# A graph layer over sorted edges: another order of loads, one-hots, clears and weight splits in the first twenty-odd microseconds

## The reference, cut to what matters

```python
h   = maximum(layernorm(x), 0)
agg = segment_sum(edge_attr, dst, 12500)        # 48 features per node
c   = concatenate([h, agg], axis=1)
h1  = silu(c  @ W1 + b1)                        # 176 -> 256
h2  = silu(h1 @ W2 + b2)                        # 256 -> 256
out = x + h + (h2 @ W3 + b3)                    # 256 -> 128
```

## Time and profile before

| | |
|---|---|
| median of 3 runs | 303.75 us |
| the profiled execution | 302.05 us |
| its span | 300.3 us |
| TensorE busy | 283.9 us (95%) |
| VectorE busy | 249.2 us (83%) |
| ScalarE busy | 222.5 us (74%) |
| GpSimd busy | 112.2 us (37%) |
| data moved | 54.49 MB, mean 181 GB/s |
| GB/s in the 7.5 us slices 1 to 6 | 171, 293, 264, 242, 170, 215 |

### The profile page before, as it was taken

The page is one execution under the profiler, slowest core; times in us unless marked ns, Lnnn a source line. Parts: engine busy times, 40 slices in busy tenths (PEclk is TensorE's granted clock), DMA queues, the critical chain, the costliest instruction groups (busy, mean ns, idle before and its releaser), DMA issues.

```text
span 300.3 us, 12188 instructions
## 1 busy us (share of the span) xinstructions
PE 283.9 (95%) x4370; PEld 256.4 (85%) x4371; DVE 249.2 (83%) x615; ACT 222.5 (74%) x434; POOL 112.2 (37%) x243
## 2 busy tenths in 40 slices
PE   7596879999999999999999999999999999999995
PEld 3584758899999999999999999999999999999794
DVE  7956988799888898889988898889988889875551
ACT  5555267887788877888777887888777887789662
POOL 4062345243433435334343334434444343542200
PEclk9899599999999999999999999999999999999999
DMA  6998999368655786557855678556875568631112
GB/s 171 293 264 242 170 215 253 85 204 244 192 164 156 228 244 177 161 158 237 243 162 151 182 240 233 157 155 189 244 232 151 150 203 244 199 109 34 33 32 58
DMA packets 79418, 54.49 MB, mean 181 GB/s; under 512 B 2997, under 2 KB 78863, under 8 KB 79253
## 3 DMA queue, kind: packets, MB, share of 16 engines
q1 hardware_dynamic: 79397, 54.25, 64.9%
HBM read 46.29 MB, written 6.40 MB: 175 GB/s over the span
## 4 chain that ended last, share of the span: by engine, by line
PE 78%; issue 8%; ACT 4%; POOL 3%; DMA 2%; DVE 1%; POOLq 1%; SPq 1%; ACTq 0%; DVEq 0%
PE agg_ps L1054 18%; PE z L1122 16%; PE z L1104 7%; PE z L1105 7%; PE z L1108 7%; PE agg_ps L1057 4%; PE z L1084 4%; PE z L1089 3%; PE z L1085 3%; PE z L1086 3%; PE z L1090 3%; POOL agg_carry L462 3%; PE tp L1068 3%; DMA raw<-in_edge_attr_dram 2%; ACT xn L543 1%
## 5 line engine op out<-in xcount | busy, mean ns | idle before, releaser
L462 POOL TENSOR_TENSOR agg_carry<-staged,agg_carry 48x42 f32 x196 | 69.5, 354 | 91.4 <-ACT staged L511 58.3
L1054 PEld LDWEIGHTS agg_ps<-onehot,raw 128*48 128x48 f32 x1560 | 75.2, 128 | 12.6 <-issue 12.5
L1054 PE MATMUL agg_ps<-onehot,raw 128*48 128x42 f32 x1560 | 78.9, 218 | 3.9 <-DVE onehot L729 3.7
L1057 PE MATMUL agg_ps<-onehot,raw 128*48 128x42 f32 x1568 | 79.3, 218 | 0.6 <-DMA raw<-in_edge_attr_dram 0.6
L729 DVE TENSOR_TENSOR onehot<-window,rel 128x1176 f32<-128x1176 f32 (+1 forms) x57 | 76.9, 1350 | 3.0 <-DVE stats L704 2.7
L1057 PEld LDWEIGHTS agg_ps<-onehot,raw 128*48 128x48 f32 x1568 | 75.8, 129 | 0.8 <-issue 0.8
L443 POOL TENSOR_TENSOR rstd<-vareps,minus_half 112x4 f32<-112x4 f32 (+1 forms) x28 | 39.5, 1411 | 77.4 <-DVE vareps L714 77.4
L1122 PE MATMUL z<-w,h 128*112 128x128 f32 (+1 forms) x448 | 55.9, 278 | 0.8 <-ACT h L575 0.8
L1122 PEld LDWEIGHTS z<-w,h 128*112 128x112 f32 (+1 forms) x448 | 50.4, 176 | 2.4 <-ACT z L571 1.1
L575 ACT ACTIVATE h<-z,b2c 128x448 f32<-128x448 f32 (+1 forms) x56 | 35.4, 633 | 20.3 <-PE z L1108 17.7
L543 ACT ACTIVATE xn<-x_t,nmr,rstd 112x128 f32<-112x128 f32 (+1 forms) x112 | 45.6, 478 | 0.9 <-DVE nmr L722 0.8
(11 more groups left out here) (128 smaller groups left out, 421.6 us busy)
## 6 DMA issues: line engine op xcount, KB each, us to landing
raw<-in_edge_attr_dram SPq DMA_DIRECT2D x55, 672.0 KB, 6.0
x_t<-in_x_dram SPq DMA_DIRECT2D x27, 224.0 KB, 6.3
out_dram<-out_t SPq DMA_DIRECT2D x27, 224.0 KB, 6.1
agg_carry<-agg_carry SPq DMA_DIRECT2D x3, 504.0 KB, 12.8
dst_rows<-in_dst_dram SPq DMA_DIRECT2D x1, 512.0 KB
raw<-in_edge_attr_dram SPq DMA_DIRECT2D x1, 288.0 KB, 3.5
dst_rows<-in_dst_dram SPq DMA_DIRECT2D x1, 256.0 KB, 2.8
out_t<-in_L_gnn_W_dram SPq DMA_DIRECT2D x1, 256.0 KB, 7.4
```

The costliest lines, as they stand in the source:

```text
L462: pool.tensor_tensor(into, staged[:, parity, n, :], into, ALU.add).then_inc(s_added, 1)
L1054: mm = pe.matmul(banks[0:ED, bass.ds(offsets[at - first], WINDOW)], edges, into, start=False, stop=True, skip_group_check=True, tile_posit ...
L1057: mm = pe.matmul(stage[ROW2:ROW2 + ED, at * WINDOW:(at + 1) * WINDOW], edges, into, start=(at == 0 and j == 0), stop=True, skip_group_chec ...
```

## The change

Ten edits, all in the beginning:

1. SP loads both halves of batch 0's edges ahead of index blocks 1 to 3; half 1 came behind them.
2. W1's loads stay where they were, W2's load moves behind the second half of batch 1's edges and the second tile of `x`, and each has its own semaphore.
3. The three copies of zeros (L384) go. GpSimd clears 16 more tiles of `agg_carry` in 4 memsets of 1,792 columns, right behind its last `iota` (L436), and ScalarE clears the last 10 with the overhang in one operation of 4,544 columns in place of two (2,752 and 896).
4. GpSimd reads the node numbers of batches 0 and 1 ahead of its first add, adds all 7 staged groups of batch 0, then computes the first `rstd`, then adds batch 1, then computes the second `rstd`. Before, `rstd` 0 came after 3 adds, and batch 1 was read and added in step 1, behind `rstd` 1.
5. VectorE makes both one-hots of batch 1 right behind those of batch 0, ahead of the check.
6. TensorE runs 5 warm-up products between the first offsets and the sum of batch 0, and turns index block 1 behind that sum and not ahead of it; 8 warm-up products, not 6, stand ahead of the sum of batch 1.
7. ScalarE copies the staged sums of batch 0 ahead of `rel_of(1)`; the high part of W2 is split behind the first normalisation.
8. VectorE splits W1's low part ahead of the first shift and W2's in step 1, behind the one-hots of batch 2.
9. The statistics of tile 1 are taken ahead of step 1; the second half of batch 2's one-hots comes ahead of the shift.
10. The waits for W2 and for the constants stand at their first users.

```diff
-    WARM0, WARM1 = 3, 6
+    WARM0, WARM1, WARM2 = 3, 5, 8
...
-        COPIED, COPIES = 6 * TILE, 3
-        ZEROED = 4 * TILE
+        ZEROED = 18 * TILE
+        CARRY0 = 2 + (ZEROED - POOL_ZEROS) // (4 * TILE)
...
-            load_edges(0, 0, 0)
+            for half in range(2):
+                load_edges(0, 0, half)
             sp.dma_start(dst_rows[:, 1:FULL_ROWS, :], rows[:, 1:FULL_ROWS, :]).then_inc(s_dst, 16)
...
-            load_edges(0, 0, 1)
             load_x(0, 0)
             load_edges(1, 1, 0)
-            sp.dma_start(w2_in, W2.rearrange("(m p) n -> p m n", p=P)).then_inc(s_weights, 16)
...
             load_edges(1, 1, 1)
+            load_x(1, 1)
+            sp.dma_start(w2_in, W2.rearrange("(m p) n -> p m n", p=P)).then_inc(s_w2, 16)
...
-            for c in range(COPIES):
-                sp.dma_start(zeros_to[:, c, :], agg_carry[:, ZEROED + COPIES * COPIED:NT * TILE]).then_inc(s_carry0_dma, 16)
...
             pool.iota(tile_i[:, :], pattern=[[1, TILE]], base=0, channel_multiplier=0).then_inc(s_pool_zero, 1)
+            for a in range(POOL_ZEROS, ZEROED, 4 * TILE):
+                pool.memset(agg_carry[:, a:a + 4 * TILE], 0.0).then_inc(s_carry0, 1)
...
             pool.wait_ge(s_off0, 1)
-            nodes = nodes_of(0)
-            pool.wait_ge(s_carry0, 2)
-            add_staged(0, 0, nodes, range(0, EARLY))
+            nodes = [nodes_of(b) for b in range(2)]
+            pool.wait_ge(s_carry0, CARRY0)
+            pool.wait_ge(s_carry0_act, 1)
+            add_staged(0, 0, nodes[0])
             rstd_of(0, 0)
-            add_staged(0, 0, nodes, range(EARLY, HALF))
+            add_staged(1, 1, nodes[1])
             rstd_of(1, 1)
...
-            clear_carry(ZEROED + COPIES * COPIED, NODES)
+            clear_carry(ZEROED, NODES)
...
-            clear_carry(POOL_ZEROS, ZEROED)
-            rel_of(1)
             stage_sums(0, 0)
-            for c in range(2, ROWS):
+            for c in range(1, ROWS):
                 rel_of(c)
...
             normalize(0, 0)
+            act.wait_ge(s_w2, W2_LOADS)
+            act.activation(w2_hi ...).then_inc(s_w_hi, 1)
             stage_sums(1, 1)
...
             make_onehot(0, 0, 1)
+            for half in range(2):
+                make_onehot(1, 1, half)
             dve.wait_ge(s_relrows, FULL_ROWS)
...
             aggregate_stats(0, 0)
-            make_onehot(1, 1, 0)
+            weights1_lo()
             shift_of_norm(0, 0)
-            make_onehot(1, 1, 1)
...
-            weights_lo()
+            load_stats(1, 1)
             dve.wait_ge(s_rel, ROWS)
...
                     agg_lo(0)
-                    load_stats(1, 1)
                     dve.wait_ge(s_stats, 2)
                     aggregate_stats(1, 1)
                     make_onehot(2, 0, 0)
+                    make_onehot(2, 0, 1)
+                    weights2_lo()
                     shift_of_norm(1, 1)
-                    make_onehot(2, 0, 1)
...
             pe.wait_ge(s_off0, 1)
+            for _ in range(WARM1):
+                pe.matmul(tp[:, 0:P], ident[:, :], ident[:, :], start=True, stop=True)
             offsets = offsets_of(0)
-            turn_rows(1)
             sum_tile(0, 0, offsets)
-            for c in range(2, ROWS):
+            for c in range(1, ROWS):
                 turn_rows(c)
...
-            for _ in range(WARM1):
+            for _ in range(WARM2):
                 pe.matmul(tp[:, 0:P], ident[:, :], ident[:, :], start=True, stop=True)
             sum_tile(1, 1, offsets)
```

More of the change, by code:

```diff
@@ L144, in gnn_kernel @@
         POOL_ZEROS = 2 * TILE
-        COPIED, COPIES = 6 * TILE, 3
-        ZEROED = 4 * TILE
-        assert ZEROED + (COPIES + 1) * COPIED == NT * TILE and LOOP[0] * TILE == ZEROED
+        ZEROED = 18 * TILE
+        CARRY0 = 2 + (ZEROED - POOL_ZEROS) // (4 * TILE)
+        assert (ZEROED - POOL_ZEROS) % (4 * TILE) == 0
         gen_onehot = onehot[:, 2:4].rearrange("p s e w -> p (s e w)")[:, 0:PER * TILE].rearrange(
@@ L451, in nodes_of, with add_staged @@
                 return nodes
-            def add_staged(b, parity, nodes, which=range(HALF)):
+            def add_staged(b, parity, nodes):
                 pool.wait_ge(s_staged, b + 1)
                 wait(pool, s_carried, b)
-                if isinstance(b, int) and b == LATE_ZEROS:
-                    pool.wait_ge(s_carry0_dma, 16 * COPIES)
-                for n in which:
+                for n in range(HALF):
                     wait(pool, s_added, added(b, n))
@@ L465, in step @@
                 parity = turn % 2
-                if has(i, 0, NT):
+                if has(i, 0, NT) and not (isinstance(i, int) and i == 1):
                     nodes = nodes_of(i)
@@ L579, in activate1 @@
                 n = PER * nodes_p(t)
+                if isinstance(t, int) and t == 0:
+                    act.wait_ge(s_const, CONSTS)
                 for m in range(M):
@@ L736, in make_onehot, with weights1_lo, weights2_lo @@
                 onehot_of(i, parity, half).then_inc(s_onehot, 1)
-            def weights_lo():
-                dve.wait_ge(s_w_hi, 4)
[L741 to L747, removed]
+            def weights1_lo():
+                dve.wait_ge(s_w_hi, 3)
+                dve.wait_ge(s_pool_zero, 3)
+                for lo, whole, hi in ((w1x_lo[:, :], w1x_in, w1x_hi[:, :]),
+                                      (w1e_lo[0:ED, :], w1e_in[0:ED, :], w1e_hi[0:ED, :])):
+                    dve.tensor_tensor(lo, whole, hi.bitcast(F32), ALU.subtract).then_inc(s_w_lo, 1)
+            def weights2_lo():
+                dve.wait_ge(s_w_hi, 4)
+                dve.tensor_tensor(w2_lo[:, :, :].rearrange("p m n -> p (m n)"), w2_in.rearrange("p m n -> p (m n)"),
+                                  w2_hi[:, :, :].rearrange("p m n -> p (m n)").bitcast(F32),
+                                  ALU.subtract).then_inc(s_w_lo, 1)
             dve.wait_ge(s_rel, 1)
@@ L857, in carry_over @@
                 dve.wait_ge(s_added, added(t + 1))
-                dve.wait_ge(s_carry0_act, 2)
-                if isinstance(t, int) and t == LATE_ZEROS - 1:
-                    dve.wait_ge(s_carry0_dma, 16 * COPIES)
+                if isinstance(t, int) and t == 0:
+                    dve.wait_ge(s_carry0, CARRY0)
+                    dve.wait_ge(s_carry0_act, 1)
                 wait(dve, s_carried, t)
@@ L1076, in layer1 @@
                 if isinstance(t, int) and t == 0:
[L1077 to L1080, removed]
+                    pe.wait_ge(s_w_lo, 2)
+                    pe.wait_ge(s_w_hi, 3)
                 for m in range(M):
@@ L1095, in layer2 @@
                 n = PER * nodes_p(t)
+                if isinstance(t, int) and t == 0:
+                    pe.wait_ge(s_w_lo, 3)
+                    pe.wait_ge(s_w_hi, 4)
                 pe.wait_ge(s_h1, M * t + M)
@@ L1116, in layer3 @@
                 last = isinstance(t, int) and t == NT - 1
+                if isinstance(t, int) and t == 0:
+                    pe.wait_ge(s_const, CONSTS)
                 pe.wait_ge(s_seeded, t + (2 if last else 1))
```

25 lines of the change are left out of this document (10 added, 15 removed).

## The result

| | kernel before | changed kernel |
|---|---|---|
| median of the runs, us | 303.84 (303.45 to 305.94, 4 runs) | 307.62 (307.10 to 307.84, 4 runs) |
| ratio to before, 95% interval | | 1.0133 (1.0096 to 1.0169) |
| profiled execution, us | 302.05 | 307.84 |
| its span, us | 300.3 | 306.1 |

1.3% slower.

A forecast was written before the change was run, and what follows sets the result against it. TensorE, gapless from 60 us, bounds the kernel, so the start of layer 1 of tile 1 counts: +5.4 (late S) - 2.0 (behind S) + 1.0 (clock) = +4.4 on 303.75 gives 308.2 us; range 304.3 to 310.8.

The forecast's parts named there:

- Which stall: VectorE's index chain: its fp32 `tensor_scalar`s stand while GpSimd's four new memsets run, shifting the chain by 6.0 us.
- let in between: Rival, VectorE's index chain: VectorE gets in between two memsets; shift 4.6 us, time 306.8 us; chance 0.20.
- The sign that I had named: VectorE's index chain: L643 or L644 lasts several us and ends near 10.
- The one-hots and the check: VectorE behind the index chain: one-hot 1 of batch 0 at 15.5, check entered at 19.4, over at 22.0.
- The offset rows: TensorE ahead of batch 1's sum: start between 22.0 and 23.3, taken as 22.6, after check and turned blocks.
- S: Moment TensorE has batch 1 summed: 23.63 before, forecast 29.0, 5.4 us late, bounds 4.8 and 6.6.
- Behind S: From batch 1's sum to layer 1 of tile 1: 16.2 us for 18.2, a gain of 2.0, bounds 2.5 and 1.2.
- The base of 15.7: VectorE's order behind S: 18.2 less statistics 0.87 and waits 0.91 and 1.37, plus W2's low part 0.67.
- the wait for `rstd`: VectorE's shift behind S waits for GpSimd's adds and `rstd`: between 0 and 1.3 us, taken as 0.5.
- The gap and the clock: TensorE idle 4.2 us ahead of layer 1 of tile 1; a clock fall behind it loses 0.8 to 2.5, taken 1.0.
- The step to the median: Whole kernel: the median lies 1.7 us above the profiled execution before; the same step put on the changed kernel.
- do not stall: Rival, VectorE's index chain: memsets do not stall it; -2.1 us, 301.7 us, 300.5 if the clock stays up; chance 0.14.

The follow-up runs named there:

- e2: Changed kernel with one GpSimd memset of 7,168 columns in place of four of 1,792: 308.33 us, 1.0160 of the kernel before.
- e5: Changed kernel with GpSimd waiting for the end of VectorE's index chain before its four memsets: 300.94 us, 0.9925 of the kernel before.
- e4: Kernel before with the new clearing alone (no copies, four memsets, one ScalarE clear), all orders as they were: 306.22 us, 1.0108 of the kernel before.
- e12: Kernel before with the new clearing alone, its four memsets waiting for the end of VectorE's index chain: 301.06 us, 0.9928 of the kernel before.
- e3: Changed kernel with sixteen GpSimd memsets of 448 columns in place of four of 1,792: 303.87 us, 0.9995 of the kernel before.
- e7: e5 with tile 1's statistics ahead of step 1 and the second `rstd` ahead of batch 1's adds: 298.69 us, 0.9868 of the kernel before.
- e1: Changed kernel with its four memsets put behind GpSimd's register loads of batches 0 and 1: 304.75 us, 1.0037 of the kernel before.
- e8: e6 and e7 together: 296.75 us, 0.9813 of the kernel before.
- e6: e5 with 12 unused TensorE products ahead of layer 1 of tile 1, two looped steps written out: 298.78 us, 0.9876 of the kernel before.

## Why the prediction came right, point by point

The measured 307.62 lies in the range and 0.6 us from the forecast of 308.2, with two errors that offset each other: that the median came so close is luck. Slower came as forecast, by the mechanism named, in the form of a rival.

- **Which stall (right) and its form (wrong).** The chain did shift because of the four memsets. But the forecast took them as one block of 6.0 us; the measured shift is 10.45 - 5.88 = 4.57, which is the rival "let in between" (4.6) to the digit, with the last stalled step L658 to L661. The sign that I had named, one operation of several us that ends near 10, did not come here; it came with the single memset (e2: 5.98 us, to 10.14). I had weighed against it that in the kernel before no stall ended at a boundary between memsets. That is still so: L639 again stands from 1.84 to 3.66 across several short memsets. Why those let nobody in, and memsets of 448 and of 1,792 columns do, stays open.
- **The one-hots and the check (right in order, 1.0 early).** The one-hot at 14.50 for 15.5, the check entered at 18.38 for 19.4 and over at 20.99 for 22.0. The smaller shift gives 1.4 of it; 0.4 was lost again between the first one-hot and the first offsets, for which VectorE waited 0.51 us for TensorE, then at 1.2 GHz.
- **The offset rows (wrong limit).** I had them at 22.6, from the check and the turned blocks together, 23.3 at most. They began at 23.57, 0.3 over that bound, set by the turned blocks alone: TensorE was at 1.2 GHz until 20.9 (0.53 in 10 to 20 us), and the five warm-ups took 2.50 us, for which the second set of eight took 2.05. I had priced the cold clock, but too low by 1 us. From there on the terms held: 23.57 + 1.64 + 2.05 + 2.7 = 29.96, measured 29.98. S was 6.35 late, forecast 5.4, inside the bounds.
- **Behind S (mis-sized).** 17.17 us, forecast 16.2. The base of 15.7 was right within 0.1, the wait for `rstd` was 1.58, not 0.5, and over the upper bound of 1.3. Rows of after show why: a GpSimd add of some 0.27 us took 3.21 beside two one-hots in a row and W2's split. The term was bounded by waits of the old order, in which the longest add took 1.73 us.
- **The gap and the clock (right, 0.5 short).** The gap was 4.11 us for 4.2, the clock fell behind it, and 1.5 us were lost (6.82 - 5.34) for 1.0.
- **What was not in the sum.** From the third `carry_over` to the end the changed kernel takes 252.5 us, before 253.5. Every kernel here has one of these two values within 0.3; what sets them is open. The sum against the profiled execution is then 5.8, not 4.4: +1.0 (offset rows), +1.0 (`rstd`), +0.5 (clock), -1.0 (this).
- **The step to the median (wrong).** I carried the 1.7 us between before's profiled execution and its median over to the changed kernel. Its profiled execution lies 0.2 above its median. This error of 1.9 took back the 1.4 that the sum was short. The plain runs of the kernel before spread from 300.75 to 305.94 over all groups, those of the changed kernel by 0.7; what they differ in is not shown, since there is a profile of one. Part of it goes with the clock, whose mean is on record for each run: the 11 runs of before at 0.972 have a median of 304.7 us, the 51 at 0.976 to 0.983 303.4, the 8 above that 302.3. The profiled execution (302.05 at 0.982) is short even for its clock.
- **The rival "do not stall" (near its price, in part by luck).** e5 is that case: S at 22.99 for 22.5, a gap of 4.19 us for 4.2, and 300.94 us for 301.7. But its profiled execution, 301.69, is 1.7 over what the same terms give for one (302.05 - 2.1): the wait for `rstd` was 1.59 for 0.5 there too, and the low clock cost 2.3 (7.33 - 5.01) for 1.0.
- **The copies and the register load (argued, now likelier).** The longest register load took 6.52 us; it is 1.22 in the changed kernel (below), 1.22 in e4 and 1.23 in e12, which differ from before in the clearing alone. That it was the copies' traffic itself, and not the memory they wrote or when they came, was not tried.

The register loads of the changed kernel (duration ns min/median/max):

```profile
L443 POOLq TENSOR_LOAD <-staged_row x28: 1001/1004/1220, 14.6 to 279.9; - x28
```

## What to carry to other kernels

A clear on GpSimd is not free because GpSimd is idle: ask which VectorE operations run beside it, cut it in pieces (no loss and no gain here, e3) or put it beside operations that do not mind, as one wait did here for 2%. Where TensorE must wait just ahead of a long dense part, some throw-away products in the gap were worth some 2 us, as much as the best reordering tried (e7), and a gain that ends in a longer gap there can be taken back by the clock. Don't carry the distance of one profiled execution from its median over to another kernel.

## What was not expected of the hardware

- Beside GpSimd's memsets single-input fp32 operations on 4 columns stand (0.17 us become up to 1.52), and so does the int32 to fp32 cast of 128x3 (1.48); two-input operations do not, neither the one-hots of 1,176 columns (three in 3.95 us with memsets and without) nor those of 3 and 4 columns (0.15 and 0.16 us inside a memset in e1 and in the changed kernel), unless they stand in the queue behind a stalled one.
- The other way round, a GpSimd add of 42 columns took 3.21 us behind back-to-back two-input VectorE operations. It was not let in between them: two one-hots and W2's split ran from 33.06 to 36.33, and it ended at 36.47. Nine of the kernels have such an add of 3.2 to 3.5 us; e7 and e8, with the adds behind the `rstd`, have none over 1.3 ahead of layer 1 of tile 1.
- The number of pieces matters more than their sum: 7,168 columns cost the chain 5.5 us as one memset, 4.6 as four, 0.5 as sixteen.
- With the gaps filled or shortened the granted clock was 1.00 over the whole span of e8, from the first products on; before, it was at 1.2 GHz for two spells of about 3.4 and 6.8 us. In nine traces of fourteen a spell followed an idle time of TensorE of 3.9 to 4.2 us ahead of layer 1 of tile 1; with 1.3 us there (e6, e8) none did.
